# Cross attention: half of each unit's exponentials transposed by a DMA on SyncE's queue, key scales loaded from GpSimd's queue, float16 codes

## What is computed

```python
q = (x @ Wq + bq) * scale ; k, v = split(cond @ Wkv + bkv)
q = _fq_sym(q, axis=-1)         # 8-bit integers times a scale, per row and head
k = _fq_sym(k, axis=-1)
v = _fq_sym(v, axis=2)          # one scale per value column, over all tokens
attn = softmax(einsum('bhqd,bhkd->bhqk', q, k))
attn = _fq_unsigned(attn, axis=-1)      # integers 0..255 times max/255, per row
out = einsum('bhqk,bhkd->bhqd', attn, v) @ Wp + bp
x = x + out
```

## Time and profile before

| | us |
|---|---|
| median of 3 runs | 658.64 (657.72 to 659.9) |
| the profiled execution | 660.86 |
| its span | 659.1 |
| first start to last start of the 32 exponentials | 148.5 to 393.5 |
| SyncE's issue of the first weights of the self attention | 376.7 |
| start of the jobs, L727 | 420.2 |

### The profile page before, as it was taken

One profiled execution on the slowest core, in us unless ns is written; L12 is line 12 of the kernel. 1 busy time (PEld: TensorE's weight loads), 2 busy tenths in 40 slices (PEclk: granted clock), 3 DMA queues, 4 the chain that ended last, 5 costly groups with the idle time before them and its releaser, 6 DMA issues. The chain is left out here.

```text
span 659.1 us, 10703 instructions
## 1 busy us (share of the span) xinstructions
PE 565.8 (86%) x4315; PEld 354.3 (54%) x4318; DVE 498.1 (76%) x894; ACT 364.8 (55%) x389; POOL 44.6 (7%) x30
## 2 busy tenths in 40 slices
PE   2899999997999799889977796799999999955566
PEld 2345555534665555555554564588865555522364
DVE  2499999858999999989997982212655773699985
ACT  5525564537899698779877883102146256431233
POOL 0200000000000000000000000000000000036860
PEclk9899999997999999989987756899999999996879
DMA  8524200043334235414431895000509222010000
GB/s 325 190 65 128 64 1 1 8 168 129 129 129 160 98 131 174 145 67 173 176 129 62 291 407 244 1 0 27 229 1 394 116 83 109 0 64 1 0 1 32
DMA packets 18896, 76.67 MB, mean 116 GB/s; under 512 B 1952, under 2 KB 3104, under 8 KB 16800
## 3 DMA queue, kind: packets, MB, share of 16 engines
q1 hardware_dynamic: 18848, 76.00, 31.7%
HBM read 75.20 MB, written 0.79 MB: 115 GB/s over the span
## 5 line engine op out<-in xcount | busy, mean ns | idle before, releaser
L1035 DVE CUSTOM_DVE_ANT_0 arena<-ps,arena 128x1024 f32<-128x1024 f32 x128 | 154.2, 1219 | 16.6 <-issue 8.7
L1400 ACT ACTIVATE arena<-arena,small 128x4096 int16<-128x4096 f32 x32 | 121.7, 3804 | 0.0
L595 PE MATMUL ps<-small,arena 128*128 128x128 bf16 x1024 | 89.5, 238 | 25.8 <-ACT arena L1400 14.5
L554 PE MATMUL ps<-arena 128*128 128x512 f16 x384 | 101.9, 387 | 0.0
L595 PEld LDWEIGHTS ps<-small,arena 128*128 128x128 bf16 x1024 | 66.7, 106 | 38.3 <-ACT arena L1400 16.9
L520 PE MATMUL ps<-arena 128*128 128x512 f16 x384 | 86.4, 383 | 0.0
L1407 ACT ACTIVATE arena<-ps 128x1024 bf16<-128x1024 int16 x64 | 65.4, 1023 | 37.1 <-PE ps L595 36.8
L727 PE MATMUL ps<-arena 128*128 128x256 f32 (+1 forms) x288 | 68.8, 398 | 0.7 <-ACT arena L1470 0.7
L727 PEld LDWEIGHTS ps<-arena 128*128 128x128 f32 x288 | 56.0, 195 | 11.6 <-issue 3.3
L611 PEld LDWEIGHTS ps<-arena 128*128 128x128 bf16 x1024 | 43.5, 99 | 33.2 <-DVE arena L1055 7.3
L520 PEld LDWEIGHTS ps<-arena 128*128 128x128 f16 x384 | 37.6, 99 | 43.1 <-issue 1.6
(11 more groups left out here) (152 smaller groups left out, 814.0 us busy)
## 6 DMA issues: line engine op xcount, KB each, us to landing
arena<-key_scales SPq DMA_DIRECT2D x64, 512.0 KB, 4.5
arena<-in_ctxT SPq DMA_DIRECT2D x8, 1024.0 KB, 5.7
arena<-in_wg SPq DMA_DIRECT2D x1, 4096.0 KB, 12.1
arena<-in_wo SPq DMA_DIRECT2D x1, 4096.0 KB, 12.0
arena<-in_wu SPq DMA_DIRECT2D x1, 4096.0 KB, 21.4
arena<-in_wd SPq DMA_DIRECT2D x4, 1024.0 KB, 5.8
arena<-in_wuq SPq DMA_DIRECT2D x1, 3072.0 KB, 24.4
arena<-in_wkr SPq DMA_DIRECT2D x1, 2048.0 KB, 11.9
```

The lines of the kernel that those rows point to most:

```text
L554: last = pe.matmul(ps[:, bank, :], wv16[wpart][:, k, g * P:(g + 1) * P], ctx16[cpart][:, k, tok], start=(k == 0 and i == 0), stop=(k == KC ...
L595: last = pe.transpose(ps[:, bank, :].bitcast(BF16)[:, b * P:(b + 1) * P], p16[u % 2][:, (8 * q + b) * P:(8 * q + b + 1) * P].bitcast(BF16) ...
L1035: dve.tensor_tensor_reduce(sc[:, u % 2, i * SCW:(i + 1) * SCW], ps[:, 2 * (n % 2):2 * (n % 2) + 2, :].rearrange("p a b -> p (a b)"), skb[: ...
L1400: act.activation(p16[u % 2], sc[:, u % 2, :], ACT.Exp, bias=ebias[:, u % 2:u % 2 + 1], scale=sq[:, i:i + 1], accum_out=rsum[:, u:u + 1]).t ...
```

## The change

- **Groups 2 and 3 of a unit's blocks** are turned by one transposing DMA of SyncE's queue, from `p16` columns 2048 to 4095 straight to `pT_dma`, one buffer for even and one for odd units, with semaphores `pT_by_dma_even` and `pT_by_dma_odd`. SyncE waits for the unit's exponentials and, from unit 2 on, for the value product of the unit two before. TensorE turns two groups only; `turns` has no entries for 2 and 3.
- **The copies**: ScalarE copies group 0, VectorE group 1, one each where it was two each.
- **No conversion**: the DMA can't convert, so the integers' bits are read as float16 (n stands for n x 2^-24); the copies keep int16, `vI` is float16, and `store_out` multiplies by 2^24 as well.
- **Waits**: `values` group 2 waits for the DMA; `scale_scores` k = 2 waits for the two groups of TensorE, k = 3 for the DMA of the unit two before.
- **The key scales** are broadcast from GpSimd's queue, the same 64 DMAs in the same order with the same kind of wait, with `RING` = 4, so chunk k always takes place k.
- The second loads of `x` and `wp` stand after the transposition of unit 28, the self attention's weights after that of unit 31.

```diff
-RING = 5
+RING = 4
-        pT = at(o_pt, [32, P], BF16)
+        pT = at(o_pt, [16, P], I16)
+        pT_dma = [at(o_pt + M * (1 + b), [16, P], I16) for b in range(2)]
-        vI = at(o_vi, [32, P], BF16)
+        vI = at(o_vi, [32, P], F16)
...
-            out = [("p", s - 2, 2)]
-            if half == 1:
-                out.append(("v", g, 2))
-            out.append(("p", s - 2, 3))
-            out += [("v", g, 3)] if half == 1 else [("v", g, 0)] if half == 0 else []
+            out = [("v", g, 2), ("v", g, 3)] if half == 1 else [("v", g, 0)] if half == 0 else []
...
+            sp.wait_ge(st_sk[1], 16)
+            for u in range(UNITS):
+                sp.wait_ge(ex, u + 1)
+                if u >= 2:
+                    sp.wait_ge(pv, NCH * (u - 1))
+                sp.dma_start_transpose(pT_dma[u % 2].bitcast(F16),
+                                       p16[u % 2][:, M // 2:M].bitcast(F16)).then_inc(ld_pT[u % 2], 16)
+                if u == UNITS - 4:
...
-                pe.wait_ge(*((tact, 2 * u + q + 1) if q < 2 else (tdve, 2 * u + q - 1)))
+                if q == 0:
+                    pe.wait_ge(tact, u + 1)
+                elif q == 1:
+                    pe.wait_ge(tdve, u + 1)
+                elif q == 2:
+                    pe.wait_ge(ld_pT[u % 2], 16 * (u // 2 + 1))
+                turned = pT if q < 2 else pT_dma[u % 2]
...
-                    elif k >= 2:
-                        dve.wait_ge(tp, NCH * (u - 2) + 2 * (k - 1))
+                    elif k == 2:
+                        dve.wait_ge(tp, 2 * (u - 1))
+                    elif k == 3:
+                        dve.wait_ge(ld_pT[u % 2], 16 * (u // 2))
...
+            pool.wait_ge(xlo, ctx_extent(STEPS - 1) + 1)
+            pool.wait_ge(st_sk[0], 16)
+            for h in range(H):
+                if h == 1:
+                    pool.wait_ge(st_sk[1], 16)
+                for k in range(NCH):
+                    n = NCH * h + k
+                    if n >= RING:
+                        m = n - RING
+                        pool.wait_ge(scu, NCH * (QT * (m // NCH) + QT - 1) + m % NCH + 1)
+                    i = ORDER[k]
+                    src = sk_dram[h // HG].rearrange("(h t) p -> h (t p)", h=HG)[
+                        h % HG:h % HG + 1, i * SCW:(i + 1) * SCW]
+                    pool.dma_start(skb[:, n % RING], src.partition_broadcast(P)).then_inc(ld_skb[n % RING], 16)
```

71 lines of the change are left out of this document (26 added, 45 removed).

## The result

| | before | after |
|---|---|---|
| median, us | 658.75 (657.72 to 659.9) | 753.07 (743.64 to 760.94) |
| the profiled execution | 660.86 | 760.94 |
| its span | 659.1 | 759.1 |
| first to last start of the 32 exponentials | 148.5 to 393.5 | 147.2 to 485.1 |
| from there to the end of the span | 265.6 | 274.0 |

The change makes the kernel slower by 14%: the ratio of the times is 1.139 (1.135 to 1.143). The forecast was 655, in a range from 637 to 688.

The account below looks back on a forecast made before the run. The prediction saw TensorE, VectorE and ScalarE nearly tied in the loop, VectorE binding after the change. Profiled 660.9 - 23.1 gained + 20 for late key scales = 657.8, less 2.2 for the median: 655 us, range 637 to 688.

Parts of the forecast that it names:

- the price of the meeting: Odd-to-even passages: key loads beside the transposition land 1.75 us late, 11 x 1.75 = 19 us, plus 1.
- The upper bound, 10.5 us for one load: Late key scales: worst case, landing like the slowest key load of all, costing 11 x 5.2 = 58 us.
- the transposition is the ring: Rival: in the loop the transposition lands after 9 us, step 7.6, total 672 us (near 690 at 10.5); chance 0.25.
- Gain of the work removed, 23.1 us: Cross attention loop and its end: fewer transposes, copies and casts save 12.2 + 4.8 + 4.4 + 1.7 us.
- all hidden: Rival: key loads in the loop land by 5.3 us, total 636, up to 645 with some lateness; chance 0.27.
- The weights moved behind the last exponential, "I count 0": End of loop: next stage's weight loads, issued some 23 us later, stay covered until 420.18; cost 0.
- The transposition alone, 5.2 us: Transposing DMA in the loop: lands after 5.2 us alone, about 6.5 in the burst, just hidden.
- Float16, nothing: Codes and output store: float16 moves no more bytes, the multiplication by 2^24 rides in the store; cost 0.
- VectorE's copy without conversion, unchanged: VectorE's remaining cast in each unit becomes a copy without conversion and keeps the same time.
- GpSimd's issue: Key loads: issue takes 0.4 us more; as rival, VectorE's casts hold each load 0.69 more, 663 us, chance 0.08.
- The clock, 0.03: Rival: TensorE, less busy in the loop, falls to 1.2 GHz; total over 720 us; chance 0.03.
- Four places in the ring: Key scale loads: with four places the lead is 5.26 us, so today's loads would already stand at the edge.

Follow-up runs that it names:

- x1: Changed kernel with the key scales of the first head loaded once for all heads, the other 60 loads left out (wrong scales for heads 1 to 15); 660.46 us.
- x2: Changed kernel with a plain SyncE copy of the same 512 KB in place of the transposing DMA, nothing turned; 680.78 us.
- x5: x2 with its copy's destination in rows of 256 bytes, so that it goes in small pieces like the transposition's; 700.08 us.
- x7: x1 with VectorE's copy ahead of its second scaling and the rotary tables loaded ahead of the self attention's weights; 635.22 us.
- x3: Kernel before with four ring places, key loads on GpSimd, float16 and the moved weights, but TensorE turning all four groups; 673.54 us, ratio 1.024.
- x11: Changed kernel, a head's first two GpSimd key loads held until the even unit's exponential ends, the other two until ScalarE's copy; 740.74 us.
- x8: Kernel before with float16 and a transposing DMA for odd units 1 to 27 only, key loads in SyncE's queue with five places; 652.69 us, ratio 0.991.
- x4: Changed kernel with the key loads issued from ScalarE's queue, two behind an even unit's exponential and two at the slot's end; 697.84 us.
- x9: Changed kernel with GpSimd's key loads held until the even unit's exponential has ended, none ahead of its transposition; 737.76 us.
- x10: Changed kernel where the even unit's transposition waits for a head's first two loads to land, and the other two loads wait for it; 774.31 us.
- x6: Changed kernel with the key loads in SyncE's own queue, two ahead of the even unit's transposition and two behind it; 691.34 us.

## Why the prediction was wrong

- **The step that failed: the price of the meeting.** The prediction added up bytes at the rate of plain loads: 1.47 us of DMA share per 512 KB, so a key load late in the burst lands after 7.0 and the transposition after 6.5. Measured, with the even units' transpositions, which are the ones in the burst: 14.6 as median and 18.7 at most, and 13.2 as median for the last load. The term "11 x 1.75 = 19 us, plus 1" was of the right kind (VectorE waits for `key_scales` at the passage from odd to even, in 11 of 15 passages, and the four in long steps are covered, as foreseen) and of the wrong size: with the loads gone (x1) the loop is 103 us shorter (93 by the times of the kernels). x2 shows that the sum of bytes was right for bytes, 20 us. It didn't hold for a transposing DMA: small packets add some 19 (x5), and its kind, at these moments and beside loads of this queue, the other 53. The share of the queue in that stays open. The upper bound, 10.5 us for one load, was taken from plain loads too, and so was itself no bound. The moments were misread as well: the prediction has the transposition start 3.3 us after the first load, which is before's timing with five places; with four it is 1.4 (276.04 and 277.39), with both first loads still in flight.
- **The rival "the transposition is the ring"** had the right sign. Its sum fits in form: from unit 12's exponential to unit 14's are 25.9 us, of which 3.9 exponential, 18.7 landing, 3.3 what follows (the prediction had 6.2 for the parts other than L; they are 7.2). But this doesn't tell it from the late loads, since both land together there, the transposition at 296.10 and the last load at 296.13, and the path that it names, VectorE's fourth scaling behind the transposition, has 1.6 us of waits in the whole loop. TensorE waits for the transposition, VectorE for the loads. Its L was 8 to 10.5 at most, and its reason, many short descriptors, is not enough: 32 of them alone land after 4.3.
- **Gain of the work removed, 23.1 us.** Right in size, and not reached. x7, without key loads and with two orders mended, has 26.0 in the loop and -0.6 in the tail, and its 635.22 is the number of "all hidden" (636). With the code as changed x1 has 10.0 in the loop. What was missed is an order: the prediction summed each engine's ring (6.2, 6.41, 5.6), and left out the ring that passes through two, VectorE's copy to TensorE's value group to the next scores to VectorE. That copy was ScalarE's before and stood ahead of everything. Step 6.88, not 6.41.
- **The weights moved behind the last exponential, "I count 0".** Wrong: the tail grew by 8.4. The 23 us of cover were compared with the landing of the first weights, 7.5, which does hold (5.0 here). But a wait for the rotary tables stands ahead of all jobs, and the tables are queued behind all the weights. The prediction had named what would count, had the cover been gone, and looked at the wrong item of the queue.
- **The transposition alone, 5.2 us:** 4.3. The estimate of 2.0 us that the prediction gives beside it isn't borne out: its packets alone take 2.9 us, from 198.6 to 201.5 in x1. **Float16, nothing:** right, even steps of 7.10 in x3. **VectorE's copy without conversion, unchanged:** right, 0.69. **GpSimd's issue:** 0.53 us each while VectorE is busy 5.96 of 6.00 us (the row 250 to 256 above), so that rival's hold of the issue isn't seen. Whether the descriptors of GpSimd's queue come late in another way stays open (x11).
- **The clock, 0.03:** no cause. It is 1.00 in steps of x1 and x8 with less work for TensorE (5.89 us of 6.90 in x1), and falls in after behind the holes. (the earlier trace rows has low slices outside 22 to 24 too, 0.7 in the tenth and 0.6 in the 37th, which the prediction passed over.)
- **Four places in the ring:** counted as 5.26 us of lead against landings of 5.3, so "at the edge". x3 puts a number to it: 10.0 us of waits even without the transposition, with GpSimd's issue in it.

## What to carry to other kernels

Price a new transfer by what is in flight beside it, of what kind and how close, not by its bytes at the rate of another kind; and if no row shows that pair, say that its cost has no upper bound in the trace, instead of borrowing one. When a copy goes from one engine to another, follow the ring through both engines, not each alone; and when transfers are moved in a queue, look at the last of them that a wait asks for, since a small table behind nearly 10 MB of weights is as late as these. If two runs are to differ in one thing, read the moments of both in their traces before the difference is given to it: x11 was built to have x4's and hasn't. If a resource is good for half of the units only, use it for that half: 14 transpositions, all but the last with no load in flight when they start, bring 0.9%, 32 beside the bursts of loads cost 14%.

## What the runs showed of the hardware

- A transposing DMA of 128 x 2048 two-byte elements within the core's memory lands after 4.3 us alone and holds SyncE's queue for 1.9 us. It counts as 2080 packets ((76192 - 9632) / 32, 9632 being before's 18848 less 64 loads of 144). The same bytes as a plain copy land after 2.9 us at best.
- With plain loads of 512 KB in flight it takes longer, by how they stand around it: 14.6 us in the median with two loads of GpSimd's queue 1.6 and 0.2 us ahead and two behind, 8.3 to 8.5 with all four behind, 4.2 with the next loads kept away (after, x11, x9, x10). The loads are stretched as well, up to 16.1 us.
- With the loads in ScalarE's queue it takes 7.9 us, in SyncE's own 6.3 (x4, x6), at other moments than after's; single ones of x4 are as bad as after's, 14.2. Whether the queue matters by itself isn't settled: it would take loads from two queues at the same moments.
- With one load issued 2.1 us behind it in its own queue and none ahead, neither lands late: 4.4 and 4.3 us (x8).
- While its packets are under way, loads of GpSimd's queue issued 0.5 and 1.3 us behind it had no packet for 5.0 us from the first one's issue (x11, 281.2 to 286.2). Why isn't settled here: it would take a run in which the loads' descriptors are there before the transposition starts.
- The 16 engines moved 284 GB/s with loads alone (247 to 254 of before), 118 with a transposition alone (197.5 to 202 of x1), and 106 with both kinds under way (256 to 264 of after).
